# Five items' norms and the first item's hidden layer placed between the steps of a state space model

## The reference

```python
h = involution(x); h = concat([cls_tok, h], axis=1)
h = h + ssm_both_ways(layernorm(h))      # gelu(scan forward) + gelu(scan backward)
xf = layernorm(h).reshape(-1, 64)
H = gelu(xf @ W1 + b1)                   # 64 -> 256
probs = softmax(H @ Wg + bg)             # 8 experts
e = argmax(probs)
h = h + probs[e] * (H @ Wd[e] + bd[e])   # the chosen expert alone, 256 -> 64
```

## Time and profile before

| | |
|---|---|
| median of 3 runs | 673.88 us (671.02 to 3102.99) |
| the profiled execution | 673.67 us, its span 672.1 us |
| PE busy | 579.4 us (86%) |
| DVE busy | 504.4 us (75%) |
| POOL busy | 418.9 us (62%) |
| ACT busy | 291.2 us (43%) |
| mean granted clock of TensorE | 0.939 of 2.4 GHz |

### The profile page before, as it was taken

One profiled execution on the slowest core, in us unless ns is written; L12 is line 12 of the kernel. 1 busy time (PEld: TensorE's weight loads), 2 busy tenths in 40 slices (PEclk: granted clock), 3 DMA queues, 4 the chain that ended last, 5 costly groups with the idle time before them and its releaser, 6 DMA issues. The chain is left out here.

```text
span 672.1 us, 9756 instructions
## 1 busy us (share of the span) xinstructions
PE 579.4 (86%) x2964; PEld 434.0 (65%) x2964; DVE 504.4 (75%) x919; ACT 291.2 (43%) x822; POOL 418.9 (62%) x641
## 2 busy tenths in 40 slices
PE   0699999985556799999983399999999999999994
PEld 0477777774445687878762257777777777777672
DVE  6588888867663787888861257888888888888884
ACT  2123222324442122222225776666666666665410
POOL 0689999805552133333345318888888888888777
PEclk9999999998786899999996579999999999999997
DMA  6200000000000000000000000000000000000001
GB/s 254 49 2 0 0 2 1 0 0 1 0 1 1 1 0 1 1 0 0 0 1 1 0 1 0 17 17 16 17 17 16 17 17 16 17 17 17 17 16 32
DMA packets 13142, 9.80 MB, mean 15 GB/s; under 512 B 4524, under 2 KB 12844, under 8 KB 12844
## 3 DMA queue, kind: packets, MB, share of 16 engines
q1 hardware_dynamic: 13084, 9.29, 4.4%
q10 hardware_dynamic: 16, 0.00, 0.0%
HBM read 5.10 MB, written 4.20 MB: 14 GB/s over the span
## 5 line engine op out<-in xcount | busy, mean ns | idle before, releaser
L1369 PE MATMUL ex_pE<-ex_WdP,ex_hid 128*128 128x512 f32 x774 | 203.9, 405 | 0.0
L1369 PEld LDWEIGHTS ex_pE<-ex_WdP,ex_hid 128*128 128x128 f32 x774 | 139.2, 188 | 42.1 <-issue 11.2
L1525 DVE TENSOR_TENSOR ex_ms<-ex_pE,ex_gate 128x512 f32<-128x512 f32 x129 | 88.0, 683 | 34.8 <-PE ex_pE L1369 34.5
L1684 POOL TENSOR_TENSOR ex_s<-ex_ms 128x1024 f32<-128x1024 f32 (+1 forms) x33 | 83.3, 2525 | 42.4 <-DVE ex_ms L1525 42.0
L644 DVE TENSOR_TENSOR inv_prod<-inv_pW,m_img 128x504 f32<-128x504 f32 x144 | 91.7, 681 | 18.3 <-PE inv_pW L559 16.6
L570 PE MATMUL inv_pS<-ident,inv_prod 128*128 128x128 f32 x576 | 88.4, 276 | 5.6 <-DVE inv_prod L644 4.9
L1182 POOL TENSOR_TENSOR hT<-hT,m_M 128x512 f32<-128x512 f32 x24 | 34.4, 1448 | 93.9 <-ACT m_M L1155 93.9
L570 PEld LDWEIGHTS inv_pS<-ident,inv_prod 128*128 128x128 f32 x576 | 70.4, 141 | 28.6 <-DVE inv_prod L644 20.2
L559 PE MATMUL inv_pW<-inv_ysb,m_conv2L 98*128 98x512 f32 x144 | 70.1, 490 | 2.3 <-DVE inv_ysb L632 2.3
L1531 DVE TENSOR_TENSOR ex_hid<-ex_hidf,ex_hid 128x512 fp32r<-128x512 f32 (+1 forms) x68 | 63.2, 948 | 9.1 <-ACT ex_hid L1433 9.1
L1138 ACT CAST ssm_z<-ssm_back 128x512 fp32r<-128x512 f32 x32 | 18.3, 619 | 102.7 <-DVE ssm_back L1114 102.7
(11 more groups left out here) (234 smaller groups left out, 1048.3 us busy)
## 6 DMA issues: line engine op xcount, KB each, us to landing
m_img<-in_x SPq DMA_DIRECT2D x2, 2048.0 KB, 9.2
out<-ex_res SPq DMA_DIRECT2D x16, 256.0 KB, 2.2
WdT<-in_L_ffn_Wd SPq DMA_DIRECT2D x2, 256.0 KB
bd<-in_L_ffn_bd SPq DMA_DIRECT2D x16, 2.0 KB
W1d<-in_L_ffn_W SPq DMA_DIRECT2D x2, 64.0 KB
m_Bm<-in_L_attn_fwd_B_real SPq DMA_DIRECT2D x2, 16.0 KB, 2.0
m_Bm<-in_L_attn_fwd_B_imag SPq DMA_DIRECT2D x2, 16.0 KB, 2.0
m_Bm<-in_L_attn_bwd_B_real SPq DMA_DIRECT2D x2, 16.0 KB, 2.0
```

The costliest lines, as they stand in the source:

```text
L1369: last = nc.tensor.matmul(pE[n % 3][0:P].rearrange("p e f -> p (e f)"), hid[i % 2][value][:, h, par, 128 * j:128 * j + P], WdP[weight][:, ...
L1525: nc.vector.tensor_tensor(ms[b % NB][0:P, t % TPB, :].rearrange("p (e f) -> p e f", e=EX), pE[n % 3][0:P], gate[i % 2][0:P, t, :].unsqueez ...
L1684: nc.gpsimd.tensor_tensor(s4[0:P, 0:T], m[:, :, 0:4 * F], m[:, :, 4 * F:], ALU.add).then_inc(halved, 1)
```

## The change

What the four windows without experts did is moved. A class `Rows` holds their tiles, semaphores and operations. Items 0 to 4 are turned in, and items 0 to 3 squared and given factors, items 0 to 2 normalised, items 0 and 1 turned out, and item 0 taken through W1 and its gelu, inside `state_space`, in steps n = 8 (`FIRST`) to 15. Both experts' weights and the biases are parted there too. The tiles lie in `u`'s places of batches whose steps are over, and the PSUM banks are those of `pV`, one step's pair between being freed by DVE and being entered again. In step k = 0 POOL fills `half` and makes the parted gate weights `WgP`. All loops of the state space are written out. `squares` writes into `xn`, of which there are three, `fac` has four buffers. `experts` starts with `judge(0)`, `add_bg(0)` and `choose_best(0)` and goes straight into `window(0)`, which has `gates(0)` and `tanh(0)` put in.

```diff
@@ state_space, PE: between enter(n + 1) and leave(n) @@
+                def rows_ahead(n):
+                    pair = pV[n % 2]
+                    if n >= FIRST:
+                        pe.wait_ge(freed, n + 1)
+                    if 0 <= n - FIRST <= 4:
+                        f.turn_in(n - FIRST, pair[0])
+                    if n == FIRST + 4:
+                        nc.tensor.matmul(pair[1][:, 0:HID], g.center[:], g.W1d[:], start=True, stop=True).then_inc(f.w1_made, 1)
+                    if n == FIRST + 5:
+                        f.turn_out(pe, 0, pair[1])
+                    if n == FIRST + 6:
+                        f.hide(pe, 0, 0, pair)
+                    if n == FIRST + 7:
+                        f.hide(pe, 0, 1, pair)
+                        pe.wait_ge(f.gelued, 2)
+                        f.turn_out(pe, 1, pV[1 - n % 2][0])
@@ state_space, PE: in enter, ahead of its matmuls @@
+                    k = b * STEPS + s - 2 - FIRST
+                    if 0 <= k <= 4:
+                        pe.wait_ge(f.rested, k + 1)
+                    if k == 4:
+                        pe.wait_ge(f.w1_parted, 1)
+                    if k == 5:
+                        pe.wait_ge(f.u_made, 1)
@@ state_space, DVE: between L1104 and the scan, L1107 @@
+                    if n == FIRST + 5:
+                        v.wait_ge(f.w1_made, 2)
+                        nc.vector.tensor_tensor(f.W1P[1][:], pV[(n - 1) % 2][1][:, 0:HID], f.W1P[0][:], ALU.subtract).then_inc(f.w1_parted, 1)
+                    if n == FIRST + 6:
+                        f.low(v, 0, pV[(n - 1) % 2][1])
@@ state_space, DVE: between L1114 and the wait for ACT's high @@
+                    if 1 <= n - FIRST <= 4:
+                        f.minus_sum(v, n - FIRST - 1)
+                    if n == FIRST + 5:
+                        v.wait_ge(f.bd_high, 1)
+                        half = slice(f.TPI * EX, 2 * f.TPI * EX)
+                        nc.vector.tensor_tensor(f.bdP[half], g.bd8[half].rearrange("k t f -> k (t f)"), f.bdh[half], ALU.subtract).then_inc(f.bd_parted, 1)
@@ state_space, DVE: after the last step @@
+                for h in range(2):
+                    for par in range(2):
+                        f.part(v, 0, h, par, f.hid0[1][:, h, par, :], rot[h][:, par, :], f.hid0[0][:, h, par, :])
+                f.low(v, 1, pV[0][0])
@@ state_space, ACT: ahead of high(n + 1) @@
+                def rows_ahead(n):
+                    k = n - FIRST
+                    if 0 <= k <= 4:
+                        act.wait_ge(f.turned_in, k + 1)
+                        f.rest(k, pV[n % 2][0])
+                    if 1 <= k <= 3:
+                        f.squares(act, k - 1)
+                    if k == 4:
+                        act.wait_ge(f.w1_made, 1)
+                        nc.scalar.copy(f.W1P[0][:], pV[n % 2][1][:, 0:HID]).then_inc(f.w1_made, 1)
+                        f.normalise(act, 0)
+                        half = slice(f.TPI * EX, 2 * f.TPI * EX)
+                        nc.scalar.copy(f.bdh[half], g.bd8[half].rearrange("k t f -> k (t f)"))
+                        nc.scalar.copy(f.bdP[0:f.TPI * EX], g.bd8[0:f.TPI * EX].rearrange("k t f -> k (t f)")).then_inc(f.bd_high, 1)
+                    if k == 5:
+                        f.high(act, 0, pV[n % 2][1])
+                        f.squares(act, 3)
+                    if k == 6:
+                        gelu(0)
+                        f.normalise(act, 1)
+                    if k == 7:
+                        gelu(1)
+                        f.high(act, 1, pV[0][0])
+                        f.normalise(act, 2)
@@ state_space, POOL: ahead of the adds of step FIRST + k @@
+                def rows_ahead(k):
+                    if k == 0:
...
+                    if 1 <= k <= 3:
+                        f.factor(pool, k - 1)
+                    if k == 4:
+                        nc.gpsimd.tensor_copy(f.WdP[0][:], g.WdT[:].rearrange("p h e f -> p h (e f)")).then_inc(f.wg_high, 1)
+                    if k == 5:
+                        f.factor(pool, 3)
+                    if k == 6:
+                        pool.wait_ge(f.wg_high, 2)
+                        nc.gpsimd.tensor_tensor(f.WdP[1][:], g.WdT[:].rearrange("p h e f -> p h (e f)"), f.WdP[0][:], ALU.subtract).then_inc(f.wd_parted, 1)
@@ experts, PE @@
                 def window(i):
...
                     if more:
                         hide(i + 1, 0)
+                    if i == 0:
+                        gates(0)
...
-                nc.tensor.matmul(pH[0][:, 0:HID], g.center[:], g.W1d[:], start=True, stop=True).then_inc(w1_made, 1)
-                turn_in(0)
-                pe.wait_ge(w1_parted, 1)
-                for i in range(1 - AHEAD, ITEMS):
+                judge(0)
+                for i in range(ITEMS):
                     window(i)
```

More of the change, by code:

```diff
@@ L1 @@
+import math
 from contextlib import ExitStack
@@ L76, in add_norm, with piece @@
     def add_norm(self, nc, ctx):
-        self.u = [ctx.enter_context(nc.sbuf_tensor(f"u{n}", [128, B, 2, QUADS], F32R)) for n in range(2)]
+        self.nc, self.at = nc, nc.sbuf_base
+        ctx.enter_context(nc.sbuf_tensor("room", [128, 4 * PAIRS * 2], F32))
+        self.u = [nc.alloc_sbuf_tensor_at(f"u{n}", [128, B, 2, QUADS], F32R, offset=self.at + 16 * PAIRS * n) for n in range(2)]
+    def piece(self, name, value, b, first, shape, dt):
+        return self.nc.alloc_sbuf_tensor_at(name, shape, dt, offset=self.at + 16 * PAIRS * value + 4 * PAIRS * b + 4 * first)
 class Matrices:
@@ L1081, in _ @@
                 pe.wait_ge(start, 2)
-                batch(0, True)
-                with pe.Fori(1, B - 1) as b:
-                    batch(b, True)
-                batch(B - 1, False)
+                for b in range(B):
+                    batch(b, b + 1 < B)
             @block.vector
@@ L1122, in _ @@
                 v.wait_ge(start, 2)
[L1123 to L1125 removed]
+                for b in range(B):
                     for s in range(STEPS):
[L1127 removed]
+                        step(b, s, b == 0)
+                for h in range(2):
+                    for par in range(2):
+                        f.part(v, 0, h, par, f.hid0[1][:, h, par, :], rot[h][:, par, :], f.hid0[0][:, h, par, :])
+                f.low(v, 1, pV[0][0])
             @block.scalar
@@ L1161, in _ @@
                 high(0, 0)
-                batch(0, True, True)
-                with act.Fori(1, B - 1) as b:
-                    batch(b, False, True)
-                batch(B - 1, False, False)
+                for b in range(B):
+                    batch(b, b == 0, b + 1 < B)
             @block.gpsimd
@@ L1442, in keep_gate @@
                     nc.scalar.copy(gT[:, 0:P], pT[:, 0:P]).then_inc(gate_kept, 1)
-                def high(i):
-                    act.wait_ge(turned_out, i + 1)
-                    if i >= 2:
-                        act.wait_ge(hidden, 4 * (i - 1))
-                    nc.scalar.copy(u[i % 2][0][:, 0:cols(i)], pXU[:, 0:cols(i)]).then_inc(u_high, 1)
-                def squares(i):
-                    act.wait_ge(summed, i + 1)
-                    if i >= 2:
-                        act.wait_ge(factored, i - 1)
-                    P = rows(i)
-                    for t in range(groups(i)):
-                        last = nc.scalar.activation(sq[0:P, i % 2, t, :], hs[i % NH][0:P, t, :], ACT.Square, scale=float(F),
-                                                    bias=stat[i % 2][0:P, 0, t:t + 1], accum_out=stat[i % 2][0:P, 1, t:t + 1])
-                    last.then_inc(squared, 1)
                 def add_bg(i):
@@ L1475, in rest @@
                         act.wait_ge(reduced, NB * (i - NH + 1))
-                    P, n = rows(i), 128 * columns(i)
-                    nc.scalar.copy(hs[i % NH][0:P, 0:groups(i), :].rearrange("p t f -> p (t f)"), pXU[0:P, 0:n]).then_inc(rested, 1)
-                def normalise(i):
-                    act.wait_ge(factored, i + 1)
-                    if i >= 1:
-                        act.wait_ge(turned_out, i)
-                    P = rows(i)
-                    for t in range(groups(i)):
-                        last = nc.scalar.activation(xn[0:P, t, :], hs[i % NH][0:P, t, :], ACT.Copy, scale=fac[i % 2][0:P, 3, t:t + 1])
-                    last.then_inc(normed, 1)
-                act.wait_ge(w1_made, 1)
-                nc.scalar.copy(W1P[0][:], pH[0][:, 0:HID]).then_inc(w1_made, 1)
-                rest(0)
-                for i in range(1 - AHEAD, ITEMS):
+                    f.rest(i, pXU)
+                add_bg(0)
+                for i in range(ITEMS):
                     if there(i + 1):
                         gelu(i + 1, 0)
+                    if i == 0:
+                        tanh(0)
+                    if there(i + 1):
                         gelu(i + 1, 1)
-                    if there(i):
-                        keep_gate(i)
+                    keep_gate(i)
                     if there(i + 2):
```

(13 more changed lines are left out.)

352 lines of the change are left out of this document (202 added, 150 removed).

## The result

The changed kernel takes **642.48 us** (median of 4 runs, 641.58 to 643.57) where the kernel before takes 674.04 beside it (median of 4, the run of 3102.99 us among them). The ratio is 0.9547, with a 95% interval of 0.9507 to 0.9586. The forecast was 643. The ratio leaves the outlier out, and by it the gain is 30.5 us. Another single run of the kernel before, at 1820.63 us, is left out in the same way in the experiments.

The account below looks back on a forecast made before the run. PE and DVE nearly fill the state space, PE the experts' windows; between them 35.8 us is pipeline-filling latency. Window 1 31.8 us sooner less 0.8 for the clock gives 31.0; 673.9 - 31.0 = 642.9, said 643, range 638 to 651.

Parts of the forecast that it names:

- PE's moved work: State space, PE in steps 8 to 14: added operations make the entering of step 15 come 2.6 to 3.0 us later.
- The new waits of PE: State space: new waits met when PE comes to them; waits within steps 8 to 14 below 0.5 us, clock 1.00.
- The slower rival: State space steps 8 to 15: 2.9 us of PE idle per step drops the clock; kernel takes 699; chance 0.03.
- the rival of no change: State space steps: the 35.8 us only spread, 4 us into each of eight steps; 674; chance 0.04.
- ACT takes the lists without delay: State space, ACT's added lists of 3.3 to 5 us a step: delay taken as nothing (0 to 2 us).
- The rival of 655 us: State space: ACT becomes the bound, each of eight steps losing 1.5 us, +12; chance 0.08.
- DVE's chain: State space, DVE: low parts and 0.3 us contention start step 14 at 334.9 and step 15 at 343.8, 2.9 later.
- The last step: State space step 15, DVE: 0.3 us of POOL contention (0 to 2), last remainder at 352.5 instead of 349.25.
- The tail: State space end: hole shrinks to about 1.5 us, clock stays, 15 matmuls take 3.5; experts start 2.3 us later.
- The start of the experts: Experts: judge(0) 1.85, window 0 17.02, gates(0) 0.45, judge(1)'s wait 0.5; 0.8 us for the clock.
- the lag rival: Experts: DVE doesn't catch up, each window may lose 0.6 us, 8.4 in all; 651 to 652; chance 0.04.
- The rival of 656 us: State space: POOL holds DVE up by the shared port, +13; chance 0.05.

Follow-up runs that it names:

- Experiment 3: Changed kernel with each of the five turnings in done twice, 2.2 us more on PE: 642.58 us, ratio 0.9555.
- Experiment 4: Changed kernel with ACT's squares of items 0 to 2 taken once more into unused tiles in steps 9 to 11: 642.06 us, ratio 0.9541.
- experiment 6: Changed kernel with WdP's difference on DVE, behind its last low parts, not on POOL in step 14: 641.52 us, ratio 0.9540.
- experiment 5: Changed kernel with POOL's two WdP operations in step 11, ahead of the factor, not in steps 12 and 14: 639.53 us, ratio 0.9536.
- Experiment 7: Changed kernel with POOL's two adds of a step held back until DVE has finished the next step's remainders: 642.16 us, ratio 0.9544.
- Experiment 8: Changed kernel with filler matmuls, two kernels: nine in step 15's idle time, 641.34 us; six behind the last class columns, 642.74 us.
- experiment 1: Kernel before with the state space's loops written out on PE, DVE and ACT, nothing else: 671.67 us, ratio 0.9994.
- dve_and_clear: Changed kernel with WdP's difference on DVE and POOL's adds held back behind DVE's remainders: 641.75 us, ratio 0.9534.
- all_three: Changed kernel with WdP's operations early on POOL, nine filler matmuls in step 15 and six behind the class columns: 641.34 us, ratio 0.9534.
- hole_filled: Changed kernel with nine more matmuls of 512 columns in PE's idle time of step 15: 641.34 us, ratio 0.9551.
- wd_by_dve: Same run as experiment 6: changed kernel with WdP's difference on DVE, behind its last low parts: 641.52 us, ratio 0.9540.
- wd_early: Same run as experiment 5: changed kernel with both WdP operations in step 11 on POOL: 639.53 us, ratio 0.9536.
- adds_clear: Same run as Experiment 7: changed kernel with POOL's adds held back until DVE has taken the remainders: 642.16 us, ratio 0.9544.
- turns_twice: Same run as Experiment 3: changed kernel with each of the five turnings in done twice: 642.58 us, ratio 0.9555.
- tail_filled: Changed kernel with six more matmuls of 512 columns behind the last class columns: 642.74 us, ratio 0.9566.
- loops_out: Same run as experiment 1: kernel before with the state space's loops written out: 671.67 us, ratio 0.9994.
- squares_twice: Same run as Experiment 4: changed kernel with ACT's squares of items 0 to 2 taken twice: 642.06 us, ratio 0.9541.
- wd_in_place: Kernel before with WdP's low half written over the weights it is made from, nothing else: 673.96 us, ratio 1.0013.
- hidden_back: Changed kernel with item 0's W1, its gelus and low parts put back at the experts' start: 652.46 us, ratio 0.9692.

## Why the prediction was right

**PE's moved work: right, a little too dear.** The entering of step 15 came 2.3 us later, forecast 2.6 to 3.0. Experiment 3 shows the mechanism: 2.2 us more of PE, 2.2 us later. DVE waited 2.10 us for PE before step 13, which began 1.3 us late, forecast 1.5.

**The new waits of PE: right.** PE waited for none of them, and the clock was 1.00 until 351 us. The slower rival, idle time and a fallen clock in each step, did not occur, nor did the rival of no change.

**ACT takes the lists without delay: right.** It waited for DVE in each of steps 9 to 15, 1.05 us at least. Experiment 4 adds 8 us for 0.6. The rival of 655 us falls. Its hops of "some tenths" are not in the steps: L1315 ends at 337.38, ACT's rounding begins at 337.42.

**DVE's chain: right to step 14, then too long.** Step 14 came 2.1 us late behind DVE's own list (332.31, PE's entering having ended at 331.75), forecast 2.2. Step 15 was to come 2.9 late, again by DVE's own list and over what PE would allow, and came 1.5 late, when both were ready within 0.03 us: DVE's remainders ended at 339.89, PE's entering at 339.86. The step between took 7.6 us, and not the 8.9 of the sum. Of these 1.3 us, 1.1 are contention that went the other way. In steps 10, 11, 12 and 14 POOL's factor (the power and its small operations) keeps POOL's adds away from the remainders, and two of them take 1.30 us instead of 2.39. In steps 11 and 12 the adds then met L1300 (1.43 and 1.09 us instead of 0.69), where DVE had time, for it waited for PE next, and in step 13 L1300 took 1.34 beside `WdP`'s copy, 0.65 us more for the 0.3 of the sum. `minus_sum` cost nothing, as forecast: DVE's wait for ACT shrank from 1.21 to 0.61 us.

```profile
302.55 1.30 DVE L1324 TENSOR_TENSOR ssm_z<-ssm_back,ssm_z 128x512 fp32r<-128x512 f32 x2 [0.61 <-ACT ssm_z L1347]
```

**The last step: the mis-sized term.** "I take 0.3 in step 13 and 0.3 in step 15, between 0 and 2": the last remainder was to come 3.2 us later and came 4.5. From its start DVE's step 15 took 2.9 us longer than the step before the change, against 0.3: 2.0 for `WdP`'s difference beside L1314 (experiments 5 and 6), 0.9 for the scan. The scan's share belongs to POOL's add: it stays when the difference is gone (experiment 6), and goes when the add is over before the scan begins (experiment 5). That the fourth factor pushed the adds back is read from the timeline (its last operation ends at 340.23, the adds begin at 340.19, and their gelu was ready at 339.05); no run left that factor out. Experiment 7 held the adds back further, and in step 15 the scan still takes 2.20.

**The tail: the second mis-sized term.** "I expect the hole to shrink to about 1.5 us and the clock to stay". It was 2.52 us, because DVE was late, and the clock fell: 5.24 us instead of 3.5. Experiment 5 shows the forecast's case, with the hole at 0.65 us and 3.68 us of matmuls. The forecast also had another path end last, ACT's list until 355.6 and its gelus behind it. In fact that list was done at 354.44, and ACT waited 1.65 us for PE's late outputs before the last gelu. Together the two terms make the experts start 4.6 us later instead of 2.3.

**The start of the experts: right, with more on `judge`.** From the first matmul to window 1 it took 20.96 us; the forecast's 1.85 + 17.02 + 0.45 + 0.5 and 0.8 for the clock are 20.6. `judge` took 3.36 at the low clock, 1.4 more than at the full one (2.00), so the 0.8 was the middle of two outcomes and neither of them; `judge(1)` waited 0.16 us, and window 0 and its waits took less than thought. DVE caught up, and the lag rival falls. Experiment 8 shows the clock's part on its own.

**The loops: right** as far as experiment 1 can tell, within 2.7 us.

**POOL's port.** The rival of 656 us has its mechanism, but not its size. The Trainium skill (SBUF — State Buffer, "Who interferes with whom" and "SBUF: two separate sides") says that a VectorE instruction with two SBUF inputs contends with a GpSimd one that reads SBUF, and that one blocks fully until the other is done. For POOL's large operations the trace agrees: L1314 began at 344.29 beside the difference, which ended at 346.46, and ended itself at 347.01, 0.55 us later. For the power it does not: L1315, whose two inputs lie in SBUF, began at 336.69, inside a power that ran from 336.12 to 338.29, and took its plain 0.69 us. The prediction says that the trace of before has no such operation beside a power. For those four lines that is so, but another operation with two SBUF inputs stands there, and could have settled it:

```profile
378.99 1.64 POOL L1667 TENSOR_TENSOR ex_fac<-ex_fac,ex_half 128x8 f32<-128x8 f32 x1
380.28 0.69 DVE L1531 TENSOR_TENSOR ex_hid<-ex_hidf,ex_hid 128x512 fp32r<-128x512 f32 x1 [6.47 <-ACT ex_hid L1433]
```

The four powers of the changed kernel took 1.97 to 2.17 us; whether POOL loses those tenths to DVE no run here tests. So the rival's 13 us, which count each of POOL's operations in full, do not arise.

**How the number came out so near.** Window 1 came 28.3 us sooner, not 31.0. Two things that the forecast did not have make it up: the windows are 0.1 us shorter (1.3 us in all), and the profiled execution was 2.5 us shorter before step 8, which is scatter. The mechanism was right but for POOL's work beside DVE, for which the sum takes 0.6 us: it made step 14 shorter by 1.1 us and step 15 longer by 2.9, and by that the hole, the clock and the path at the block's end came out otherwise. That the sum is within 1 us is partly luck.

## What to carry to other kernels

Pipeline fill at the start of a stage is latency, and it can be had for nearly nothing in the stage before it if that stage is bound by another engine: here a stretch of 35.8 us became 4.6 us of longer state space and one `judge`. Count what each operation leaves in the bounding engine's list, then look at the last step by itself, for there nothing behind it absorbs a late engine. An operation on POOL that reads many elements from SBUF can cost DVE nearly its whole length (2.0 of 2.34 us here) if it meets a two-input operation there, on whichever line that is; put it where DVE has slack, since holding it back mostly changes whom it meets. And moving it to DVE is no way out when POOL still has work beside it: POOL's last add then took 1.0 us longer and ended the block.

## What the runs showed of the hardware

**A scan meets POOL too.** `TENSOR_TENSOR_SCAN` of 512 columns takes 1.28 us, 2.19 to 2.20 with a POOL add of 512 columns beside it (the change, experiment 6), and 3.32 beside a POOL subtraction of 1024 elements (experiment 3). POOL's subtraction of 1024 elements took 3.32 us beside DVE, and 2.34 alone: both sides lose.

**The clock is not decided by PE's idle time alone.** PE's idle time before the last outputs, and the time of the 15 matmuls behind it:

| kernel | idle us | 15 matmuls us | idle before `judge` | `judge` us |
|---|---|---|---|---|
| dve_and_clear | 0 | 3.57 | 3.86 | 3.59 |
| all_three | 0 | 3.57 | 0.45 | 2.01 |
| hole_filled | 0.47 | 3.69 | 1.90 | 3.25 |
| wd_by_dve | 0.61 | 3.69 | 2.86 | 3.59 |
| wd_early | 0.65 | 3.68 | 1.88 | 2.02 |
| adds_clear | 1.66 | 3.68 | 2.95 | 2.90 |
| turns_twice | 2.41 | 3.68 | 1.93 | 2.00 |
| the change | 2.52 | 5.24 | 1.36 | 3.36 |
| tail_filled | 2.56 | 5.25 | 0.45 | 2.00 |
| loops_out | 2.68 | 3.71 | | |
| squares_twice | 2.70 | 5.22 | 1.36 | 2.01 |
| before | 2.86 | 5.25 | | |
| wd_in_place | 2.86 | 5.24 | | |
| hidden_back | 4.67 | 5.63 | | |

Up to 1.66 us the clock always stayed for the outputs. Between 2.4 and 2.9 it fell five times and stayed twice, and before `judge` the same 1.36 us gave both 3.36 and 2.01. What decides between them no run here shows. A forecast should carry both ends, 1.6 us apart for the outputs and 1.4 to 1.6 for `judge`.
